# Expert stage of an RWKV-style layer with a mixture of experts: the first product of every odd tile as three fp32r products of split halves

## What is computed

```python
h = layernorm(x)                                   # 2048 x 512
combine = top-4 weights of 32 experts per row      # from h @ gate_w
up = jnp.einsum('th,ehi->tei', h, Wu)              # Wu: 32 x 512 x 256
act = relu(up) ** 2
routed = jnp.einsum('tei,te,eih->th', act, combine, Wd)   # Wd: 32 x 256 x 512
shared = relu(h @ Wsu) ** 2 @ Wsd
out = x + routed + shared
```

## Time and profile before

| | |
|---|---|
| median of 3 runs | 1094.7 us |
| the profiled execution | 1089.49 us |
| its span, first to last instruction | 1087.5 us |
| TensorE matmul busy | 1050.0 us (97%) |
| VectorE busy | 574.4 us (53%) |
| ScalarE busy | 536.5 us (49%) |
| GpSimd busy | 431.9 us (40%) |
| mean granted TensorE clock | 0.995 |
| DMA moved | 192.91 MB, 177 GB/s |

### The profile page before, as it was taken

One profiled execution on the slowest core, in us unless ns is written; L12 is line 12 of the kernel. 1 busy time (PEld: TensorE's weight loads), 2 busy tenths in 40 slices (PEclk: granted clock), 3 DMA queues, 4 the chain that ended last, 5 costly groups with the idle time before them and its releaser, 6 DMA issues.

```text
span 1087.5 us, 17100 instructions
## 1 busy us (share of the span) xinstructions
PE 1050.0 (97%) x4892; PEld 844.3 (78%) x4893; DVE 574.4 (53%) x1110; ACT 536.5 (49%) x892; POOL 431.9 (40%) x327
## 2 busy tenths in 40 slices
PE   2999999999999999999999999999999999999998
PEld 0446878888788878887887878888888888888887
DVE  7977855925390548050007497945445544454514
ACT  4634626333433333333334343357777766776742
POOL 1012303320222132211223423377777777887641
PEclk9899999999999999999999999999999999999999
DMA  8705168525532642234253891067999999987678
GB/s 282 261 1 193 58 235 307 175 78 191 177 97 78 221 164 89 88 132 155 97 206 132 302 300 58 5 196 162 280 192 259 230 234 313 208 192 140 89 175 343
DMA packets 98306, 192.91 MB, mean 177 GB/s; under 512 B 13000, under 2 KB 33480, under 8 KB 97744
## 3 DMA queue, kind: packets, MB, share of 16 engines
q1 hardware_dynamic: 79008, 151.63, 40.0%
q0 software_dynamic: 18816, 39.87, 19.4%
q10 hardware_dynamic: 432, 0.79, 0.2%
HBM read 137.78 MB, written 60.03 MB: 182 GB/s over the span
## 4 chain that ended last, share of the span: by engine, by line
PE 77%; DVE 10%; DMA 7%; issue 3%; ACT 1%; SPq 1%; POOL 1%; ACTq 0%; DVEq 0%; POOLq 0%
PE bank L613 36%; PE bank L937 21%; PE bank L1541 10%; PE bank L525 3%; DMA shx_d<-yo,idy 3%; PE bank L1533 2%; DMA res_d<-yo,idy 2%; PE bank L1549 1%; DMA hT_d<-hT 1%; DVE big L1326 1%; SPq L1060 1%; DVE mx L359 1%; DMA g1b<-in_L_attn_ln_b 1%; PE bank L948 1%; DVE bns L248 1%
## 5 line engine op out<-in xcount | busy, mean ns | idle before, releaser
L918 POOL TENSOR_TENSOR ksp_lo<-ra,ksp_hi 128x512 fp32r<-128x512 f32 x96 | 145.8, 1519 | 447.1 <-ACT ksp_hi L868 447.0
L1685 DVE TENSOR_TENSOR wds<-w,wds 128x1024 fp32r<-128x1024 f32 x84 | 103.1, 1228 | 158.8 <-ACT wds L1622 158.8
L1541 PE MATMUL bank<-w,xT 128*128 x672 | 158.8, 379 | 1.2 <-ACT xT L1606 0.8
L937 PE MATMUL bank<-vring,ksp_hi 128*128 128x512 f32 x512 | 159.4, 393 | 0.0
L860 ACT ACTIVATE ra<-bank 128x512 f32<-128x512 f32 x96 | 57.4, 598 | 177.2 <-PE bank L613 174.9
L1541 PEld LDWEIGHTS bank<-w,xT 128*128 128x128 f32 x672 | 126.9, 189 | 21.6 <-issue 1.8
L613 PE MATMUL bank<-wds,aT 128*128 128x512 f32 x504 | 137.3, 407 | 0.0
L868 ACT ACTIVATE ksp_hi<-ra 128x512 fp32r<-128x512 f32 x96 | 60.7, 632 | 124.7 <-PE bank L937 124.3
L937 PEld LDWEIGHTS bank<-vring,ksp_hi 128*128 128x128 f32 x512 | 95.5, 188 | 20.0
L613 PE MATMUL bank<-xcT_hi,wck_lo 128*128 128x512 f32 x256 | 101.7, 397 | 0.0
L613 PE MATMUL bank<-xcT_lo,wck_hi 128*128 128x512 f32 x256 | 101.5, 396 | 0.0
(11 more groups left out here) (267 smaller groups left out, 1920.6 us busy)
## 6 DMA issues: line engine op xcount, KB each, us to landing
vring<-wcv_d SPq DMA_DIRECT2D x64, 512.0 KB, 3.3
w<-in_L_ffn_Wu SPq DMA_DIRECT2D x32, 512.0 KB, 7.5
w<-in_L_ffn_Wd SPq DMA_DIRECT2D x32, 512.0 KB, 8.9
hT_d<-hT SPq DMA_DIRECT2D x16, 512.0 KB, 3.7
hTb<-hT_d SPq DMA_DIRECT2D x3, 2048.0 KB, 10.9
raw_wcv<-in_L_attn_Wcv SPq DMA_DIRECT2D x4, 1024.0 KB, 6.6
raw_wck<-in_L_attn_Wck SPq DMA_DIRECT2D x4, 1024.0 KB, 9.5
f<-in_L_attn_x SPq DMA_DIRECT2D x4, 1024.0 KB, 6.9
```

Of the source, the lines that this page charges most:

```text
L918: nc.gpsimd.tensor_tensor(ksp[1][:, i % 2], ra[:, i % 2], ksp[0][:, i % 2], ALU.subtract).then_inc(sem("klo_in"), 1)
L937: m = nc.tensor.matmul(bank[to + j][:], ksp[l][:, i % 2, j * P:(j + 1) * P], rhs(r), start=i == 0 and k == 0, stop=i == last and k == 2)
L1541: m = nc.tensor.matmul(bank[4 + u][:, 0:EI], xT4[:, u, c * P:(c + 1) * P], slot_of(wu8[:, :, c * EI:(c + 1) * EI], e), start=c == 0, stop= ...
L1685: nc.vector.tensor_tensor(wds[:, u, 1], slot_of(wd8, e), wds[:, u, 0], ALU.subtract).then_inc(sem("wl4"), 1)
```

## The change

In every odd tile but the first one (tile 1), the first product is no longer four float32 matmuls but `split_product` over four blocks of 128 rows: twelve fp32r matmuls of 256 columns. For that, each odd step has three new pieces of work and one that differs:

- `x_in` of an odd tile writes the fp32r tile `xhi` instead of a float32 copy; VectorE's `x_lo` then subtracts it from the PSUM bank into `xlo`.
- ScalarE's `wu_hi` converts the first weights of the odd tile two ahead (128 x 1024) to fp32r, placed ahead of `take_y`.
- VectorE's `wu_lo` makes their low half, placed ahead of `w_lo`; both of its inputs lie in SBUF.
- TensorE's `up_split` waits for `x_lo` and `wu_lo` (semaphores xl4, wul4), and the transposes into bank 7 wait for the `x_lo` that read it.

The owner words are read at other distances for this, and ScalarE reads one every two tiles in the main loop instead of every four. The diff, cut to what is spoken of:

```diff
@@ -201,11 +201,15 @@
         wu8, wd8 = w8[:, :, 0:C * EI], w8[:, :, C * EI:]
         XRING, YRING = 12, 4
         xg = [at(f"xg{n}", [P, H + E], F, 2.125 * (n % 6) + (186 if n < 6 else 80)) for n in range(XRING)]
-        xT4 = at("xT4", [P, 2, C * P], F, 180.5)
+        xT4 = at("xT4", [P, C * P], F, 180.5)
+        xhi = at("xhi", [P, C * P], R, 182.5)
+        x1 = at("x1", [P, C * P], F, 201.5)
         a4 = at("a4", [P, 2, EI], F, 92.75)
         aT4 = at("aT4", [P, 2, 2, EI], R, 164.5)
         yo = at("yo", [P, YRING, H], F, 172.5)
         wds = at("wds", [P, 2, 2, EI // P * H], R, 64)
+        wus = [at(f"wus_{s}", [P, C * EI], R, kb) for s, kb in (("hi", 160.5), ("lo", 168.5))]
+        xlo = at("xlo", [P, C * P], R, 201.5)
         idc = at("idc", [P, GROUP], I32, 199.5)
         idy = at("idy", [P, GROUP], I32, 199.625)
@@ -1508,12 +1512,36 @@
                                              max_val=(1 << OWNER_BITS * PACK) - 1)
                 yield k, (word >> OWNER_BITS * j) & E - 1, (word >> OWNER_BITS * (j + 2)) & E - 1
...
+        def odd_count(i, t):
+            return GROUP // 2 * i + (t - 1) // 2
         def x_count(i, t):
             return 16 * i + 16 * (t // XRING) + 16
-        def first_owners(engine, n):
-            return [e for _, e in owners(engine, 0, n)]
+        def first_owners(engine, n, first=0):
+            return [e for _, e in owners(engine, first, n - first)]
         def slot_of(ring, e):
             return ring[:, bass.ds(e & WSLOTS - 1, 1)].rearrange("p a n -> p (a n)")
@@ -1529,6 +1557,8 @@
                 s = t % XRING
                 pe.wait_ge(sem(f"xg_in{s}"), x_count(i, t))
                 pe.wait_ge(sem("xt4"), GROUP * i + t + 1)
+                if u and t > 3:
+                    pe.wait_ge(sem("xl4"), odd_count(i, t - 2))
                 for c in range(C):
                     m = nc.tensor.transpose(bank[6 + u][:, c * P:(c + 1) * P], xg[s][:, c * P:(c + 1) * P], ident[:])
                 m.then_inc(sem("t4"), 1)
@@ -1538,9 +1568,17 @@
                 pe.wait_ge(sem("xt4"), g + 3)
                 pe.wait_ge(sem("r4"), g + 1)
                 for c in range(C):
-                    m = nc.tensor.matmul(bank[4 + u][:, 0:EI], xT4[:, u, c * P:(c + 1) * P],
+                    m = nc.tensor.matmul(bank[4 + u][:, 0:EI], (xT4, x1)[u][:, c * P:(c + 1) * P],
                                          slot_of(wu8[:, :, c * EI:(c + 1) * EI], e), start=c == 0, stop=c == C - 1)
                 m.then_inc(sem("u4"), 1)
+            def up_split(i, t):
+                pe.wait_ge(sem("xl4"), odd_count(i, t))
+                pe.wait_ge(sem("wul4"), odd_count(i, t))
+                pe.wait_ge(sem("r4"), GROUP * i + t + 1)
+                xs4 = (xhi, xlo)
+                split_product(bank[5][:, 0:EI], lambda s, c: xs4[s][:, c * P:(c + 1) * P],
+                              lambda s, c: wus[s][:, c * EI:(c + 1) * EI], C).then_inc(sem("u4"), 1)
             def turn(g, u):
                 pe.wait_ge(sem("s4"), g + 1)
@@ -1558,7 +1596,10 @@
             def step(i, t, e, more=True):
                 g, u = GROUP * i + t, t % 2
-                up(g, u, e)
+                if u:
+                    up_split(i, t)
+                else:
+                    up(g, u, e)
                 if more:
                     tin(i, t + 2, u)
                 turn(g - 1, 1 - u)
@@ -1600,10 +1641,15 @@
             down3(pe, NSI - 1)
         def stage4_scalar(act):
-            def x_in(g, u):
+            def x_in(g, u, split=False):
                 act.wait_ge(sem("t4"), g + 1)
                 act.wait_ge(sem("u4"), g + 1)
-                nc.scalar.activation(xT4[:, u], bank[6 + u][:], ACT.Copy).then_inc(sem("xt4"), 1)
+                to = xhi if split else (xT4, x1)[u]
+                nc.scalar.activation(to[:], bank[6 + u][:], ACT.Copy).then_inc(sem("xt4"), 1)
+            def wu_hi(e):
+                wait_apart(act, sem("win"), e + 1)
+                nc.scalar.activation(wus[0][:], slot_of(wu8, e), ACT.Copy).then_inc(sem("wuh4"), 1)
             def relu(g, u):
                 act.wait_ge(sem("u4"), g + 3)
@@ -1629,18 +1675,21 @@
                 nc.scalar.activation(yo[:, t % YRING], bank[u][:], ACT.Copy,
                                      scale=xg[t % XRING][:, bass.ds(H + e, 1)]).then_inc(sem("y4"), 1)
-            def step(i, t, before, e, more=True, first=False):
+            def step(i, t, before, e, ahead, more=True, first=False):
                 g, u = GROUP * i + t, t % 2
                 relu(g, u)
                 if more:
-                    x_in(g + 2, u)
+                    x_in(g + 2, u, split=u)
                 a_hi(g - 1, 1 - u)
+                if more and u:
+                    wu_hi(ahead)
                 take_y(i, t - 2, u, before, first)
                 w_hi(g, u, e)
             act.wait_ge(sem("owner_in"), 1)
             passes = passes_of(act)
             early = first_owners(act, YRING + 2)
+            ahead = first_owners(act, YRING + 4, first=YRING + 2)
             act.wait_ge(sem("kc_in"), N4)
             w_hi(0, 0, early[0])
             x_in(0, 0)
@@ -1650,19 +1699,21 @@
             relu(0, 0)
             x_in(2, 0)
             relu(1, 1)
-            x_in(3, 1)
+            x_in(3, 1, split=True)
+            act.wait_ge(sem("klo_in"), N4 + 2)
+            wu_hi(early[3])
             a_hi(0, 0)
             act.wait_ge(sem("bs_st"), 16 * NB)
             for t in range(2, YRING + 2):
-                step(0, t, early[t - 2], early[t], first=True)
+                step(0, t, early[t - 2], early[t], (early + ahead)[t + 2], first=True)
             with act.Fori(0, PASSES - 1) as i, act.If(i < passes):
-                for k, before, e in owners_apart(act, GROUP * i + YRING + 2, GROUP):
-                    step(i, YRING + 2 + k, before, e)
+                for k, before, e, ahead in owners_around(act, GROUP * i + YRING + 2, GROUP):
+                    step(i, YRING + 2 + k, before, e, ahead)
             n = GROUP - YRING - 2
-            for k, before, e in owners_apart(act, GROUP * passes + YRING + 2, n + 2):
+            for k, before, e, ahead in owners_around(act, GROUP * passes + YRING + 2, n + 2):
                 t = YRING + 2 + k
                 if k < n:
-                    step(passes, t, before, e, more=k < n - 2)
+                    step(passes, t, before, e, ahead, more=k < n - 2)
                 else:
                     if k == n:
                         a_hi(GROUP * passes + GROUP - 1, 1)
@@ -1684,26 +1735,42 @@
                 dve.wait_ge(sem("wh4"), g + 1)
                 nc.vector.tensor_tensor(wds[:, u, 1], slot_of(wd8, e), wds[:, u, 0], ALU.subtract).then_inc(sem("wl4"), 1)
-            def step(g, u, e):
+            def x_lo(i, t):
+                dve.wait_ge(sem("xt4"), GROUP * i + t + 3)
+                nc.vector.tensor_tensor(xlo[:], bank[7][:], xhi[:], ALU.subtract).then_inc(sem("xl4"), 1)
+            def wu_lo(i, t, e):
+                dve.wait_ge(sem("wuh4"), odd_count(i, t))
+                nc.vector.tensor_tensor(wus[1][:], slot_of(wu8, e), wus[0][:], ALU.subtract).then_inc(sem("wul4"), 1)
+            def step(i, t, e, ahead, more=True):
+                g, u = GROUP * i + t, t % 2
                 square4(g, u)
+                if u and more:
+                    x_lo(i, t + 2)
                 a_lo(g - 1, 1 - u)
+                if u and more:
+                    wu_lo(i, t + 2, ahead)
                 w_lo(g, u, e)
             dve.wait_ge(sem("owner_in"), 1)
             passes = passes_of(dve)
-            early = first_owners(dve, 2)
+            early = first_owners(dve, 4)
             w_lo(0, 0, early[0])
             w_lo(1, 1, early[1])
             square4(0, 0)
             square4(1, 1)
+            x_lo(0, 3)
+            dve.wait_ge(sem("vc_done"), N4 + 2)
+            wu_lo(0, 3, early[3])
             a_lo(0, 0)
             with dve.Fori(0, PASSES - 1) as i, dve.If(i < passes):
-                for k, e in owners(dve, GROUP * i + 2):
-                    step(GROUP * i + 2 + k, k % 2, e)
-            rest = GROUP * passes
-            for k, e in owners(dve, rest + 2, GROUP - 2):
-                step(rest + 2 + k, k % 2, e)
-            a_lo(rest + GROUP - 1, 1)
+                for k, e, ahead in owners_ahead(dve, GROUP * i + 2, GROUP):
+                    step(i, 2 + k, e, ahead)
+            n = GROUP - 2
+            for k, e, ahead in owners_ahead(dve, GROUP * passes + 2, n):
+                step(passes, 2 + k, e, ahead, more=k < n - 2)
+            a_lo(GROUP * passes + GROUP - 1, 1)
         HALF_PASS = GROUP // 2
 
```

More of the change, by code:

```diff
@@ L1509, in owners_apart, with owners_ahead, owners_around @@
                 yield k, (word >> OWNER_BITS * j) & E - 1, (word >> OWNER_BITS * (j + 2)) & E - 1
+        def owners_ahead(engine, g, n):
+            for k in range(n):
+                j = k % (PACK - 2)
+                if j == 0:
```

(18 more changed lines are left out.)

## The result

The change made the kernel slower: 1106.9 us median of 4 runs (1102.7 to 1107.8) against 1093.6 of before, a ratio of 1.0114, with a 95% interval of 1.0084 to 1.0144. The forecast was 1091.3 and "same"; the measured time lies just inside the slow end of the range of 1081 to 1107. The profiled execution took 1107.8 us (span 1105.7), 18.3 above that of before, which was one of the quick ones of its kernel.

What follows compares the result with a forecast made beforehand. The prediction took GpSimd's scatter chain, close beside TensorE's step, to decide the expert stage. Terms of -1.9, -6.5 and +5 gave -3.4 us from 1094.7, so 1091.3 us; the range was 1081 to 1107.

Steps and rivals of the forecast that it cites:

- Two chains side by side: Expert stage: TensorE's step, 3.77 us per tile, and GpSimd's scatter chain, 3.95, run close together; the second decides.
- a ring that is full sooner: Four output tiles between ScalarE's copy and GpSimd's scatter: distance from copy to scatter at 7.5 us by tile 20 to 25.
- copies that wait for landings well above 23.5 us: Sign of being right: ScalarE's output copies wait for DMA well above the 23.5 us of before.
- the second direction of the rule: GpSimd's SBUF reads holding VectorE's two-SBUF-input operations: wu_lo held up to 1.6 us, TensorE's gain shrinking by up to 12.
- The price of a pair: TensorE's split product: 0.115 us per fp32r pair, ends 0.111 and 0.189; 0.35 us saved per odd tile, 14.4 in all.
- ScalarE's added work at nothing: ScalarE's extra 1.05 us conversion per odd tile, ahead of the output copy, fits in idle time: costed at nothing.
- step (ii): Tiles without late landings: GpSimd's scatters come at TensorE's pace, so 37 tiles gain 0.175 us each, -6.5 us.
- step (iii): GpSimd starts held by wu_lo, the third long blocking operation per pair of tiles: +5 us, between 0 and 11.5.
- rival B: GpSimd: from a full ring on, scatters run into wu_lo and are held; slower, 1105 to 1113 us; chance 0.22.
- a held start shortens the next wait for a landing: GpSimd: the argument against the slower rival, whose chance was 0.22; no size of its own was given.
- (i): Behind tile 72, no more gathers and GpSimd catches up: 11 tiles, each 0.175 us shorter on average, -1.9 us.
- TensorE did wait, which I had costed at nothing: TensorE waiting for its split operands: costed at nothing, and named as a sign of being wrong.

Runs made afterwards that it cites:

- e10: The changed kernel with the expert stage's 84 scatter-adds left out, a two-element memset standing for each: 1077.9 us, ratio 0.9827 to the kernel before.
- e4: The kernel before with one extra ScalarE conversion of 128x1024 per odd step ahead of the output copy, result unused: 1095.5 us, ratio 1.0023.
- e9: The kernel before with the expert stage's 84 scatter-adds left out, a two-element memset standing for each: 1088.2 us, ratio 0.9934.
- e1: The changed kernel with wu_lo subtracting from a PSUM bank instead of the weight slot, so one SBUF input (values wrong): 1094.2 us, ratio 1.0008 to the kernel before.
- e8: The changed kernel with all splits and waits, but the odd tiles' first product again one float32 product: 1110.7 us, ratio 1.0131 to the kernel before.
- e6: The kernel before with its long subtraction w_lo (second weights' low half) in two pieces of 512 columns: 1091.9 us, ratio 0.9956.
- e5: The changed kernel with both long subtractions, w_lo and wu_lo, in two pieces of 512 columns each: 1101.4 us, ratio 1.0034 to the kernel before.
- e3: The kernel before with an extra 128x1024 VectorE subtraction per odd step, one input in PSUM, result unused: 1100.2 us, ratio 1.0051.

## Why the prediction was wrong

**Right.** Two chains side by side, with a ring that is full sooner, and copies that wait for landings well above 23.5 us (48.7). That x_lo out of PSUM holds nobody (5 starts, 0.01 us). That wu_lo holds starts and is itself never held: L1744 takes 1.21 to 1.25 us throughout, so the second direction of the rule in the Trainium skill (SBUF — State Buffer, Who interferes with whom) is again not seen, and the first is. The price of a pair, 0.120 us, lay between the ends but above the 0.115 taken; per odd tile it is 0.28 instead of 0.35, 11.5 us in 41 tiles instead of 14.4, and e10 collects 10.3 of them. The Trainium skill (TensorE: Matmul & The Clock Gate, Back-to-back issue gap) gives N / 2.4 + 2.5 ns for an isolated matmul, an estimate of 0.109 us with 256 columns; the pairs of this trace are further apart. ScalarE's added work at nothing is nearly right: e4 has 2.5 us (0 to 5) against it, and where the ring is free e9 and e10 show none of it (the copies of tiles 3 to 72 gain 10.3 us, where 0.28 in each odd tile makes 9.7).

**Wrong, step (ii).** "Where no landing is late [...] the scatters come at TensorE's pace [...] There a faster TensorE helps", -6.5 us. It does not. e1 has the faster product and no held scatters, and its chain is 275.6 us against 272.3; e8 has the slow one and all the holds, and its time is that of the changed kernel. The argument took a stretch in which GpSimd falls in step with the rest as one in which TensorE leads. But a scatter gains from an earlier copy only if it waits for one, and it did not. These are all its waits for a copy from 740 to 1034 us in the kernel before (us, times, longest):

```profile
POOL res_d L1733 <- ACT yo L1629: 3.7, 6, 2.2
POOL shx_d L1733 <- ACT yo L1629: 0.6, 2, 0.3
```

The one of 2.2 lies behind tile 72. The seven up to there are of 0.31 us, the pause that GpSimd makes before most scatters whatever they wait for, and from tile 4 to 72 the scatter starts 1.9 us or more behind its copy. So the 6.5 us had nothing to come from; a faster TensorE only comes sooner to a full ring. A sign of it stood in the rows used: 3.95 us a tile on GpSimd against TensorE's free 3.77 over the same 69 tiles.

**Wrong, step (iii).** +5 us for the starts that wu_lo holds, between 0 and 11.5. Measured are 15.0, and 3.1 more for index copies, which I had not counted among the starts at all. The upper end was itself too low, because it scaled the count of held starts by the number of blocking operations (half as many again) at the same loss each. In fact 31 starts fell into wu_lo, where half of 51 is 26, and they lose more: its 17 scatters 0.66 us each, where a start in w_lo lost 0.45 on average before (23.1 / 51). Six of the 17 come 0.05 us behind its beginning, as in the row above, and lose 1.04 to 1.06 each; rival B had said "a scatter some 0.3 later runs into it".

**Wrong, the weighting.** What happened is rival B, in its place and its mechanism: a ring full sooner (after 19 tiles; measured by tile 13) and scatters that run into wu_lo. Its 1105 to 1113 holds the 1106.9, but in part by luck: B let a scatter be held in each of 34 pairs, though by its own reckoning the ring is full for only some 25 of them, and 17 scatters and 14 gathers were held. The whole range holds the time only because it reaches into B. B was given 0.22, with the argument against it that a held start shortens the next wait for a landing. e6 shows that argument at work (10.3 us of holds are worth 1.4 us of chain), e5 and e1 where it ends: with wu_lo the holds are more than the landings can hide. (i), -1.9 behind tile 72, gave -0.6.

TensorE did wait, which I had costed at nothing, though not for its split operands: its transposes of the activation (L1587) waited 18.6 us in 12 waits for the square, where it was 3.4 us in 6 before, and its second product 4.0 us in 9 waits for a_lo. From 740 to 1034 us:

```profile
PEld bank L1587 <- DVE a L1727: 18.6, 12, 5.6
```

One of them, on the timeline and the table by stretch (PE, PEld, DVE, ACT, POOL, clock, DMA share, GB/s):

```profile
902.46 0.69 ACT L1675 ACTIVATE yo<-bank,xg 128x512 f32<-128x512 f32 x1 [5.03 <-DMA shx_d<-yo,idy]
```

```profile
905.91 0.22 PEld L1587 LDWEIGHTS bank<-ident,a 128*128 128x128 f32 x1
...
907.21 0.33 PEld L617 LDWEIGHTS bank<-wds,aT 128*128 128x128 f32 x1
907.63 0.33 PEld L617 LDWEIGHTS bank<-wds,aT 128*128 128x128 f32 x1
```

```profile
900.00:905.00 5.00, 2.56 (x19) 2.19 (x18) 0.76 (x1) 2.54 (x6) 2.29 (x3) 1.00 1.08 313
905.00:910.00 5.00, 4.14 (x14) 3.43 (x15) 4.17 (x8) 4.33 (x9) 4.08 (x4) 0.66 0.96 216
```

The copy waits 5.03 us for a landing; the ReLU, its square and so TensorE's transposes queue behind it, TensorE stands still for 3.5 us, and then the granted clock drops: 0.66 on average from 905 to 910, with the second product's loads 0.42 us apart, twice the 0.21 of full speed, so at 1.2 GHz. Four such drops lie between 740 and 1034 us (mean clock 0.97; before 1.00), none in e9 and e10, where TensorE never stands still for as long as 1.5 us. They can have cost this kernel little: GpSimd waited only 2.0 us for a copy in that stretch, so TensorE had the time. That they are a sign of the full ring and not the cause of the loss is read from this, no run shows it by itself.

## What to carry to other kernels

Before an engine is made faster, sum the other chain over the same tiles with everything in it (issues, holds, waits for landings); if it is already the longer one, the gain stays in the buffers. Ask of each stretch whether the slower engine waits for the faster one at all. An operation with two SBUF operands on VectorE had a price on GpSimd's DMA starts here, which no busy share shows: ask whether one operand can come from PSUM, or try it in pieces (of 512 columns they helped, of 256 they made it worse). Estimate what it may hold by where the starts fall, not by how many operations there are, and try an edit that only changes the rhythm before believing a count.

## What the runs showed of the hardware

- A start of a gather, scatter or index copy on GpSimd was held by a VectorE operation with two SBUF operands until about 0.12 us before its recorded end (71 held starts of the changed kernel; 48 in w_lo lost 21.4 us); with one operand in PSUM, at the same 1.21 us, 34 starts (e1) and 28 (e3) lost no more than 0.03 us each.
- Back-to-back pieces of 256 columns (0.42 us, one every 0.335) hold a start over many seams, up to 2.6 us; pieces of 512 (0.69 us, one every 0.60) mostly let it in at the first (one gather of e5 lost 1.37, all else 0.52 or less).
- An fp32r pair with 256 columns comes every 0.120 us, where half of the 512-column pair would be 0.114.
- The times of the same kernel spread by a little over 1% (before: 1087.6 to 1101.1 in 28 runs) and go with the mean granted clock, which was 0.991 to 0.998: about 1.2 us for each 0.001.
- TensorE stood still for 3.5 us from 902.3 us on in the changed kernel, and its granted clock was then 0.5, at 1.2 GHz, for 3.4 us; three more drops to 0.5 lie between 740 and 1034 us, and none in e9 and e10, where TensorE never stood still for as long as 1.5 us in that stretch.
